# The modulation of two adaLN layers spread over three later stages, and row statistics taken by chunk inside the projections

## What is computed

```python
mod = (_silu(L0_c) @ L0_wmod).reshape(L0_c.shape[0], 6, 1, -1)
sa, ca, ga, sb, cb, gb = (mod[:, 0], mod[:, 1], mod[:, 2], mod[:, 3], mod[:, 4], mod[:, 5])
ga = (2 * (ga >= 0) - 1) * jnp.maximum(jnp.abs(ga), 0.25)
gb = (2 * (gb >= 0) - 1) * jnp.maximum(jnp.abs(gb), 0.25)
```

## Time and profile before

| | us |
|---|---|
| median of 3 runs | 2526.34 (2525.19 to 2531.87) |
| the profiled execution | 2524.06 |
| its span | 2522.3 |
| around the span | 1.8 |

### The profile page before, as it was taken

The page is one execution under the profiler, slowest core; times in us unless marked ns, Lnnn a source line. Parts: engine busy times, 40 slices in busy tenths (PEclk is TensorE's granted clock), DMA queues, the critical chain, the costliest instruction groups (busy, mean ns, idle before and its releaser), DMA issues. The chain is left out here.

```text
span 2522.3 us, 39140 instructions
## 1 busy us (share of the span) xinstructions
PE 2205.9 (87%) x12968; PEld 1402.0 (56%) x12968; DVE 1698.6 (67%) x2697; ACT 1274.8 (51%) x2451; POOL 870.0 (34%) x1055
## 2 busy tenths in 40 slices
PE   3786899999999999998799789963999999999991
PEld 1674233333333333325677556642888888888881
DVE  4784878788777878855688768864455555555456
ACT  1232377677767777775233244421455555555453
POOL 2355123131212312112455422445344434444341
PEclk8897799999999999999899889985999999999996
DMA  4259702240404220003000100014443433453326
GB/s 173 95 160 181 101 2 33 38 68 3 69 3 69 26 45 2 2 1 105 1 0 0 33 0 1 34 38 166 156 158 135 137 130 130 153 174 136 133 72 212
DMA packets 126576, 200.18 MB, mean 79 GB/s; under 512 B 13696, under 2 KB 98688, under 8 KB 124992
## 3 DMA queue, kind: packets, MB, share of 16 engines
q1 hardware_dynamic: 108976, 140.13, 16.6%
q0 software_dynamic: 15600, 52.25, 11.0%
q10 hardware_dynamic: 1824, 5.52, 1.3%
HBM read 150.97 MB, written 46.88 MB: 78 GB/s over the span
## 5 line engine op out<-in xcount | busy, mean ns | idle before, releaser
L907 DVE TENSOR_REDUCE tile_max<-p_m 128x2 f32<-128x1024 f32 (+3 forms) x640 | 651.1, 1060 | 143.7 <-PE p_m L769 75.2
L869 ACT ACTIVATE probs<-p_s 128x512 f32<-128x512 f32 (+3 forms) x1280 | 597.0, 535 | 241.7 <-PE p_s L778 236.7
L2093 PE MATMUL p_up<-f_xT,f_w 128*128 128x512 f32 (+1 forms) x2304 | 463.4, 351 | 8.8 <-POOL f_w L2256 8.8
L2093 PEld LDWEIGHTS p_up<-f_xT,f_w 128*128 128x128 f32 x2304 | 368.7, 189 | 59.1 <-issue 9.2
L715 POOL TENSOR_SCALAR_AFFINE_SELECT probs<-probs 128x128 f32<-128x128 f32 x512 | 145.0, 292 | 718.5 <-ACT probs L869 709.7
L765 PE MATMUL p_m<-ka,qa 96*128 96x512 bf16 (+3 forms) x1280 | 362.2, 366 | 30.9 <-PEq L330 18.8
L2256 POOL TENSOR_TENSOR f_w<-f_raw,f_w 128x1024 fp32r<-128x1024 f32 x96 | 231.5, 2415 | 399.0 <-ACT f_w L2145 399.0
L778 PE MATMUL p_s<-qa,ka 99*128 99x512 bf16 (+3 forms) x1280 | 352.6, 352 | 18.2 <-ACT probs L869 6.9
L792 PE MATMUL p_o<-probs,va 128*32 128x512 f32 (+3 forms) x2560 | 300.6, 541 | 0.3 <-POOL probs L715 0.3
L2108 PE MATMUL p_y<-f_w,f_hidden 128*128 128x256 f32 x1872 | 255.8, 283 | 28.8 <-DVE f_hidden L2210 14.9
L2108 PEld LDWEIGHTS p_y<-f_w,f_hidden 128*128 128x128 f32 x1872 | 237.3, 188 | 50.6 <-issue 31.5
(11 more groups left out here) (251 smaller groups left out, 2579.7 us busy)
## 6 DMA issues: line engine op xcount, KB each, us to landing
f_raw<-in_W1a SPq DMA_DIRECT2D x24, 1024.0 KB, 6.7
f_raw<-in_W1b SPq DMA_DIRECT2D x24, 1024.0 KB, 9.0
f_raw<-in_W SPq DMA_DIRECT2D x24, 1024.0 KB, 11.3
qk_scr<-parts SPq DMA_DIRECT2D x48, 256.0 KB, 2.5
qa<-qk_scr POOLq DMA_DIRECT2D x42, 256.0 KB, 15.4
ka<-qk_scr POOLq DMA_DIRECT2D x42, 256.0 KB, 17.1
v_scr<-wqkv_raw SPq DMA_DIRECT2D x32, 256.0 KB, 3.3
g_ys<-y_rows SPq DMA_DIRECT2D x16, 512.0 KB, 8.7
```

The costliest lines, as they stand in the source:

```text
L869: nc.scalar.activation(probs[:, (buf * UNITS + n) % NPROBS, h, lo:CH], p_s[:, s_bank(("exp", HG * n + h), buf), lo:CH], ACT.Exp, scale=DH ...
L907: nc.vector.tensor_reduce(out=tile_max[:, 2 * hp:2 * hp + 2, i, bank], in_=p_m[:, at_bank, :, 0:width], op=ALU.max, axis=AX.X).then_inc(ma ...
L2093: last = nc.tensor.matmul(p_up[:, f % 2, ab, 0:size], w1[:, wh, ab * KT + kt, f * P:(f + 1) * P], xT[:, t % 2, xh, kt, 0:size], start=(kt, ...
```

## The change

The stage `modulation` is gone. Its parts now stand in three places.

1. Layer 0's modulation, the constants and the statistics are in `projections`. SP issues, in this order: c, the first third of wmod0, x of chunk 0, the identity, the projection weights, x of chunk 1, the masks, the rest of wmod0, cos and sin, x of chunks 2 to 7. The scratch for it lies in `qa0` and `va0`, the products go to the bank of the values. PE makes two products, then two more, transposes chunk 0, and makes the last two. DVE takes the statistics of chunk 0, then of chunk 1, and those of chunk i+2 at the end of chunk i; POOL raises each chunk's four columns to -1/2 between `add(i, 1)` and `split_off(i, 1)`; norm(i) waits for it. The low parts of the weights go from POOL to DVE. The loops over the middle chunks are written out.
2. Layer 1's c and wmod are loaded in `output_projection`, where ACT takes silu(c) before its first `copy` and DVE makes `cb`. The six products stand at the start of `top1_experts`, before the first transpose, with ACT's copies; DVE adds 1 before its last `finish`.
3. `guard_gates` runs for layer 0 at its old place and for layer 1 in `layer1`, on DVE after the first `invert` ops.

```diff
@@ sync, projections
-                sp.dma_start(raw[:, :, :], a["wqkv"].rearrange("(k p) n -> p k n", p=P)).then_inc(w_loaded, 16)
+                sp.dma_start(cT, a["cT0"]).then_inc(c_loaded, 16)
+                sp.dma_start(wm[:, :, 0:2 * D], wm_src[:, :, 0:2 * D]).then_inc(wm_loaded[0], 16)
+                load_x(0)
+                sp.dma_start(k.ident[:, :], a["ident"]).then_inc(constants_loaded, 16)
                 sp.dma_start(raw[:, :, :], a["wqkv"].rearrange("(k p) n -> p k n", p=P)).then_inc(w_loaded, 16)
+                load_x(1)
+                sp.dma_start(masks, a["masks"]).then_inc(constants_loaded, 16)
+                sp.dma_start(wm[:, :, 2 * D:6 * D], wm_src[:, :, 2 * D:6 * D]).then_inc(wm_loaded[1], 16)
                 sp.dma_start(trig[:, :, :], a["trig"]).then_inc(trig_loaded, 16)
...
@@ gpsimd, projections
                 def chunk(i, par):
-                    for qk in range(2):
-                        add(i, qk)
-                        split_off(i, qk)
-
-                root(nc, pool, k, 0)
-                pool.wait_ge(k.rstd_ready, 1)
+                    add(i, 0)
+                    split_off(i, 0)
+                    add(i, 1)
+                    if i + 2 < NCH:
+                        deviation(i + 2)
+                    split_off(i, 1)
...
                 nc.gpsimd.memset(k.ka0[QROWS:QROWS + SPLIT, :, :], 1.0).then_inc(ones0_set, 1)
                 pool.wait_ge(ones0_set, 1)
-                for n, cols in enumerate(columns):
-                    pool.wait_ge(w_high, n + 1)
-                    nc.gpsimd.tensor_tensor(w[:, LO, :, cols], raw[:, :, cols], w[:, HI, :, cols], ALU.subtract
-                                            ).then_inc(w_ready, 1)
-                all_chunks(pool, chunk)
+                deviation(0)
+                deviation(1)
+                all_chunks(chunk)
@@ vector, projections
+                def statistics(i):
+                    dve.wait_ge(x_in[i], 16)
+                    for t in range(i * TPC, (i + 1) * TPC):
+                        c.add(nc.vector.bn_stats(out=k.stats[:, t, :], in_=k.x[:, t, :]))
+                    aggregate_rows(nc, c, k, rows_of(i)).then_inc(ve_ready, 1)
...
                     rotate(i, 1)
+                    if i + 2 < NCH:
+                        statistics(i + 2)
@@ scalar, output_projection
                 keep(0)
                 keep(1)
+                act.wait_ge(c_loaded, 16)
+                nc.scalar.activation(ew.silu_c[:, :, :], ew.cT[:, :, :], ACT.Silu).then_inc(c_ready, 1)
@@ tensor, top1_experts
+                for n in range(len(halves)):
+                    modulate(n)
                 turn(0, 0)
                 choose(0, 0)
+                pe.wait_ge(mod_copied, len(halves))
@@ vector, layer1
+                guard_gates(nc, k.mods[1], c_own, *(y_sb[:, 0, f, :].rearrange("p (b d) -> p b d", b=B) for f in range(2)))
```

More of the change, by code:

```diff
@@ L227, with guard_gates @@
-NORM_STEPS = TPC + 1
-AGGREGATE_STEPS = 6
+def guard_gates(nc, mods, own, sign, mag):
+    for which in (GA, GB):
+        gate = mods[:, :, which, :]
+        own.wait()
+        own.add(nc.vector.tensor_scalar(sign, gate, 0.0, 2.0, ALU.is_ge, ALU.mult))
+        own.step(nc.vector.scalar_tensor_tensor(out=mag, in0=gate, scalar=-1.0, in1=gate,
+                                                op0=ALU.mult, op1=ALU.max))
+        own.step(nc.vector.tensor_scalar(mag, mag, 0.25, None, ALU.max))
+        own.step(nc.vector.scalar_tensor_tensor(out=gate, in0=sign, scalar=-1.0, in1=mag,
+                                                op0=ALU.add, op1=ALU.mult))
@@ new lines, in aggregate_rows @@
+def aggregate_rows(nc, own, k, rows):
+    (mean_e, m2_e), (mean_o, m2_o) = ((k.stats[:, rows, i], k.stats[:, rows, i + 1]) for i in (1, 4))
+    mean, ve, spread = k.mean[:, rows], k.ve[:, rows], k.spread[:, rows]
+    own.wait()
+    own.add(nc.vector.tensor_tensor(mean, mean_e, mean_o, ALU.add))
+    own.add(nc.vector.tensor_tensor(spread, mean_e, mean_o, ALU.subtract))
+    own.step(nc.vector.tensor_tensor(ve, m2_e, m2_o, ALU.add))
+    own.add(nc.vector.tensor_scalar(mean, mean, 0.5, None, ALU.mult))
+    own.add(nc.vector.tensor_scalar(ve, ve, 1.0 / D, EPS, ALU.mult, ALU.add))
+    own.step(nc.vector.scalar_tensor_tensor(out=spread, in0=spread, scalar=0.25, in1=spread, op0=ALU.mult, op1=ALU.mult))
+    return nc.vector.tensor_tensor(ve, ve, spread, ALU.add)
@@ L1122, in top1_experts @@
         own = m.sem("c_own")
+        mod_product, mod_copied, mods_ready = m.sem("c_mod_product"), m.sem("c_mod_copied"), m.sem("c_mods_ready")
+        halves = [(b, half) for b in range(B) for half in range(3)]
         PICKS = 3
@@ L1161, in tile @@
                                             ).then_inc(half_ready, 1)
-                root(nc, pool, k, 1)
+                root(nc, pool, k)
                 scale(0, 0)
@@ L1293, in _ @@
                 all_tiles(dve, tile)
+                dve.wait_ge(mod_copied, len(halves))
+                for which in (CA, CB):
+                    nc.vector.tensor_scalar(k.mods[1][:, :, which, :], k.mods[1][:, :, which, :], 1.0, None, ALU.add).then_inc(mods_ready, 1)
                 finish(NT - 1, 1)
```

254 lines of the change are left out of this document (127 added, 127 removed).

## The result

The changed kernel takes **2504.09 us** in the median (2501.4 to 2507.85, four runs) against 2527.23 of the kernel before (2525.19 to 2531.87, four runs): a ratio of 0.9909, 95% interval 0.9893 to 0.9924. The direction was right and the size was not: 23 us came off where 32 were forecast, and the median is just outside the range. (One execution of a later variant, `e_best`, was disturbed, 2857.95 us, its profiled one; that variant's times here are of its five other runs.)

What follows compares the result with a forecast made beforehand. A serial head (first transpose at 68.61 us), then a DVE, POOL and ACT ring setting the chunk period, bound the kernel. Terms -48.1 + 13.2 - 2 + 3.9 + 0.6 = -32.4 gave a median of 2494 us, range 2484 to 2504.

Steps and rivals of the forecast that it cites:

- Head, -48.1: Program start: first transpose 49.1 us earlier, less what a later norm(1) costs; -48.1 us.
- the first rival: Program start: POOL's memset does not hold `cb`, the first chunk comes 4 us sooner; 2490 us, chance 0.12.
- another rival: Program start: loads sharing SP's queue arrive at half rate, h's transpose waits 5 us; 2499 us, chance 0.05.
- Chunks, +2.2 each: Projections: statistics before six norms wait for POOL's add, +2.2 us a chunk, +13.2 in all.
- the rival "slower": Projection chunks: idler PE gets 1.2 GHz and becomes the bound, +10.6 us a chunk, up to 2568; chance 0.03.
- Tail, -2: End of projections: one of six chunk delays falls between attention's loads and is given back; -2 us.
- in attention the ops that go had cover: Attention: the removed ops had cover, so their removal was set at 0.
- Output projection, +3.9: Output projection: first copy waits for c and silu, first product +2.9 us, slower matmuls +1; +3.9 us.
- Experts, +0.6: Experts' start: six products put the transpose +3.9 us later, but warm PE saves on matmuls; +0.6 us.
- if it falls in the middle +3: Experts' start: case where PE's clock falls midway, making the term +3 us.
- Layer 1 and combine, 0: Layer 1: eight guard ops lie ahead of a DVE wait of 12.36 us and are free; 0 us.
- The clock rival: Output projection, experts and head: PE gets 1.2 GHz in all three, 1.6, 2.4 and 2 to 3 us more; 2500, chance 0.14.

Runs made afterwards that it cites:

- e_best: Changed kernel with statistics in VectorE's idle slot, cT first in the output projection's queue and the experts' tiles written out; median 2471.25 us.
- e_memset_split: Changed kernel with GpSimd's starting memset cut into four, one behind the first add of chunks 0 to 3; 2505.78 us, one run.
- e_stats_slot: Changed kernel with the statistics moved before the first split, where VectorE idles, and GpSimd's power behind its first add; median 2487.43 us.
- e_loads_early: Changed kernel with attention's first-stage loads issued behind chunks 4 and 5 instead of 4, 5 and 6; 2508.7 us, one run.
- e_c_first: Changed kernel with cT loaded first instead of fourth on the output projection's SyncE queue; 2492.96 us, one run.
- e_all: e_best plus memset in four pieces, chunk 0's transpose behind two products instead of four, two layer 1 products behind the experts' last tile; median 2474.59 us.
- e_final: e_all without the cut of the memset; median 2474.19 us.
- e_best_again: e_best once more, unedited, for a profile of its stages; 2468.43 us, one run.
- e_five: e_best with two of layer 1's six products behind the experts' last tile; median 2469.48 us.
- e_silu_late: Changed kernel with the output projection's silu moved behind the copy of chunk 3 and the `cb` writes behind VectorE's last chunk; 2499.75 us, one run.
- e_before_again: The kernel before, unedited, run again for a second profile of attention; 2525.09 us, one run.

## Why the prediction was right in direction and wrong in size

**Head, -48.1: right.** -48.96. The memset held `cb` to 8.43 (8.8 forecast), the transpose came at 19.36 (19.55), and `e_memset_split` shows that the first rival's 4 us would not have come: wmod0 was the next wait. Nor did sharing one queue hold the head, as another rival had it: PE waited 0.92 us for a load. That the two agree to 0.9 us is in part luck, since in nine profiles with the same code up to chunk 0's first product this add ended at 44.4 to 46.0 us.

**Chunks, +2.2 each: right.** 2.28 each, 3.26 us from the add to the second norm op, period 20.56 (20.4). The sum set the unrolled loops at 0; by `e_stats_slot` the statistics cost 2.38 each, and the written-out chunks gave 0.6 us back in all. The rule that the prediction took from the Trainium skill ("SBUF — State Buffer", Who interferes with whom) is borne out by the row of 2.08 us: the trace agrees that a two-input op waits for a GpSimd instruction that reads.

One reading under the rival "slower" was wrong: "80% busy kept 1.00" came from one stretch. In the kernel before the clock already stood at 0.50 from 127.5 to 130.9 and from 182.1 to 185.5, and in the changed one it does so for 3.4 us in each of the six periods with statistics (PE's busy time, clock and DMA, kernel after):

```profile
115.00:118.00 3.00, 3.00 (x8) 0.50 0.09 31
```

It cost nothing here: in `e_loads_early` the first two periods are without such a stretch and take 20.57 and 20.59 us, the next two have one and take 20.55. PE does not set the period.

**Tail, -2: wrong, -0.25.** The step that failed is "one of the six delays falls between these loads and is given back". ScalarE waited 6.96 us as before. The loads are issued by ScalarE itself chunk by chunk, so they were delayed with the chunks: from the first issue of the last third to the end of ScalarE's wait it is 16.08 us before (205.92 to 222.00) and 16.03 after (170.65 to 186.68). As I read it, they pressed on the stores as they had.

**Attention, "in attention the ops that go had cover": right but for 0.28 us, as far as is known.** +2.75 in the pair; 0.28 of it goes with the change, the rest is within the scatter of 10 us shown by the profiles. The anchor was part of this: the profiled execution of before had the shortest attention of all fifteen.

**Output projection, +3.9: right mechanism, too small.** +5.18. The first product came 3.67 us later, not 2.9, since the silu began 5.68 us behind c's issue (1127.82 to 1133.50), and the remaining 1.5 us, which I put down to half clock, had been set at 1. The table load of 1.28 us was not in the sum; it lies under the wait. `e_c_first` took away all but 0.2.

**Experts, +0.6: the step that failed.** Of the 4.24 us, 2.4 are the start. The transpose came as forecast, but "PE is then warm: the first twelve expert matmuls take 3.13 instead of 5.47" did not hold; they took 4.59, and the gain of 2.34 us became one of 0.9. The case "if it falls in the middle +3" was named and not chosen. (By the mean of 0.83 in the earlier trace rows the clock fell at 1202.7 and not at 1202.8, which changes nothing.) Thirteen profiles tell when it falls: none of the five with cT first (`e_c_first`, `e_all`, `e_final`, `e_best_again`, `e_five`) shows the second fall (6.5 us from the pick of tile 0 to that of tile 1), the eight others all do (8.0 us). It is not the speed of the output projection before it: `e_silu_late` had its first product sooner than `e_c_first` (4.70 against 5.18 us) and a stage of 43.64 against 43.38, and still fell. What else parts the two groups in the traces is when the clock rose behind the start of the products: 3.3 to 4.4 us into the stage in the five, 5.2 to 6.2 in the eight. Whether that decides it, and by what rule, these runs do not show. The other 1.9 us, the growth with the loop, had no term in the sum: the code of the loop was untouched and I set it at nothing. PE's waits for `c_hT` behind the turns grew from 2.8 to 4.5 us in all.

**Layer 1 and combine, 0:** +0.74, in a stretch that took 1082.5 (`e_before_again`) to 1085.5 us (`e_five`) in all profiles; nothing to explain.

The head alone came out better than forecast, by 0.9 us; all other misses went the other way: 1.4 (start to attention, the head included), 2.7, 1.3, 3.6 and 0.7 us make the 9.8 between the forecast difference and that of the spans. The clock rival (2500) comes nearest in time and only in part for its reasons: its 2 to 3 us at the head did not come, of its 1.6 on the output projection 0.5 did (the rest of that miss is the later first product), and of its 2.4 on the experts 1.8. What fills its sum is the loop, the tail and the scatter of attention, and that is luck.

## What to carry to other kernels

When a stage is dissolved into others, its work costs what the slot costs in which it lands: the same statistics cost 2.4 us a chunk in front of the norm and nothing in VectorE's wait for ScalarE, and a 2 KB load cost 5.0 us more where it was issued fourth than where it was first. Before moving work out of an engine's way, find the next wait (the memset's hold hid one for wmod0), and do not empty the gap in which an engine waited, if what filled it then stands on the path. Price TensorE's restart after each idle gap by both clocks, and compare one execution with another only by stages, since one stage here scattered by 10 us.

## What the runs showed of the hardware that I had not expected

- A loop over tiles on all engines costs more than its turn: 6.47 us a tile written out, 6.71 and 7.09 in the loop, 11 us in 32 tiles. PE, which never waits in the first case, idles 0.22 to 0.34 us behind each turn in the second.
- The granted clock fell in tile 0 of the experts, to 0.50 from 1190.1 to 1193.5, behind some 8 us of products at full clock with a wait of 1.2 us between; it did so in eight of eight profiles without cT first and in none of the five with it.
- In nine profiles with the same code up to there, PE's first product starts at 8.49 us in all, but the granted clock rose to 1.00 between 11.5 and 14.5 us, and the later it rose, the later chunk 0's first product of queries began (23.2 to 24.7).
- Two profiles of the same kernel differ by a clock of 0.83 against 1.00 over the same 20 us of attention, with PE as busy in both (18.07 and 18.05 us); in fifteen profiles the stage's length ranged from 927.1 to 937.2 us.
- GpSimd's memset, which only writes, stretched four 128x128 TENSOR_SCALARs from 0.87 to 5.46 us.
